# A fused four-stage network kernel: its first attention stage written anew with four heads per step

## What is computed

```python
Q = (x @ WQ_w.T + WQ_b).reshape(b, sq, 16, 16).transpose(0, 2, 1, 3)   # K, V from kv
T = einsum('bhqd,bhkd->bhqk', Q, K) / 4 + attn_bias[:, None]
T = where(mask_i * mask_j == 0, -1e9, T)
out = einsum('bhqk,bhkd->bhqd', softmax(T), V)
x = x + tanh(g_xattn[0]) * (out @ WO_w.T + WO_b)
```

## Time and profile before

| | us |
|---|---|
| median of 3 runs | 2507.8 |
| lowest, highest | 2505.95, 2511.61 |
| the profiled execution | 2495.91 |
| its span | 2493.9 |
| start of A's first scores block | 53.8 |
| B's first load | 469.56 |

### The profile page before, as it was taken

One profiled execution on the slowest core, in us unless ns is written; L12 is line 12 of the kernel. 1 busy time (PEld: TensorE's weight loads), 2 busy tenths in 40 slices (PEclk: granted clock), 3 DMA queues, 4 the chain that ended last, 5 costly groups with the idle time before them and its releaser, 6 DMA issues. The chain is left out here.

```text
span 2493.9 us, 47660 instructions
## 1 busy us (share of the span) xinstructions
PE 2239.0 (90%) x17920; PEld 1548.8 (62%) x18016; DVE 1748.6 (70%) x4970; ACT 879.7 (35%) x2051; POOL 147.6 (6%) x236
## 2 busy tenths in 40 slices
PE   3888888697999999999789999999779999999998
PEld 1555566444475575668445655555568888888887
DVE  4878778476665656553677777777578787878785
ACT  1767567305032131230455555555321111111110
POOL 1623511000000000000000000000000000000000
PEclk8999999799999999999899999999999999999999
DMA  7345233300000000200100000000300000000000
GB/s 195 65 80 88 49 48 48 136 0 1 1 1 1 1 1 1 102 1 1 45 1 1 1 1 1 1 1 1 126 11 1 2 8 0 0 8 0 0 9 9
DMA packets 43512, 65.33 MB, mean 26 GB/s; under 512 B 5056, under 2 KB 36160, under 8 KB 42688
## 3 DMA queue, kind: packets, MB, share of 16 engines
q1 hardware_dynamic: 43328, 62.88, 10.6%
HBM read 54.48 MB, written 8.39 MB: 25 GB/s over the span
## 5 line engine op out<-in xcount | busy, mean ns | idle before, releaser
L2608 PEld LDWEIGHTS banks<-work,big 128*128 128x128 f32 x2048 | 249.7, 194 | 9.7 <-issue 1.9
L2608 PE MATMUL banks<-work,big 128*128 128x128 f32 x2048 | 251.6, 277 | 1.9 <-ACT work L2699 1.7
L2181 PE MATMUL banks<-big,work 128*128 128x256 f32 x1024 | 241.2, 379 | 3.6 <-issue 3.3
L2715 ACT ACTIVATE work<-banks 128x512 f32<-128x512 f32 x128 | 76.5, 598 | 434.1 <-PE banks L2608 434.1
L2107 PE MATMUL banks<-big,work 128*128 128x512 f32 x512 | 221.4, 593 | 0.0
L1791 ACT ACTIVATE work<-banks,work 128x512 f32<-128x512 f32 x256 | 174.1, 686 | 122.0 <-DVE work L1880 121.9
L2181 PEld LDWEIGHTS banks<-big,work 128*128 128x128 f32 x1024 | 195.0, 190 | 33.9 <-issue 1.9
L888 ACT ACTIVATE work<-work 128x512 f32<-128x512 f32 x256 | 182.8, 716 | 83.4 <-DVE work L1026 83.4
L771 PE MATMUL banks<-ident,work 128*128 128x128 f32 x1024 | 161.9, 282 | 49.9 <-ACT work L888 45.2
L1026 DVE CUSTOM_DVE_ANT_0 work<-banks,big 128x512 f32<-128x512 f32 x256 | 173.1, 686 | 38.6 <-issue 34.1
L771 PEld LDWEIGHTS banks<-ident,work 128*128 128x128 f32 x1024 | 122.6, 143 | 83.9 <-ACT work L888 56.1
(11 more groups left out here) (211 smaller groups left out, 3928.0 us busy)
## 6 DMA issues: line engine op xcount, KB each, us to landing
wc<-parts SPq DMA_DIRECT2D x128, 128.0 KB, 6.4
parts<-big SPq DMA_DIRECT2D x16, 384.0 KB, 2.5
big<-in_bias SPq DMA_DIRECT2D x4, 1024.0 KB, 9.7
big<-in_B_val SPq DMA_DIRECT2D x8, 512.0 KB, 6.9
big<-in_B_out SPq DMA_DIRECT2D x1, 4096.0 KB, 19.8
big<-in_D_downT SPq DMA_DIRECT2D x1, 4096.0 KB, 13.8
big<-in_D_up SPq DMA_DIRECT2D x1, 4096.0 KB, 23.1
wc<-in_ctxT SPq DMA_DIRECT2D x1, 2048.0 KB, 7.9
```

Of the source, the lines that this page charges most:

```text
L2181: last = eng.matmul(XO[qt // 2][:, qt % 2 * D:(qt % 2 + 1) * D], spread[:, c % NG, qt * P:(qt + 1) * P], w_out[:, c, :], start=False, stop ...
L2608: last = eng.matmul(HP[n % 2][:, q * P:(q + 1) * P], down[:, kc * ELO + n * NJ + q, :], xnT[par][:, kc, :], start=(kc == 0), stop=(kc == K ...
```

## The change

The prologue block, `cross_attention`, the unused `moe_attention` and `turns` go; `a_attention` takes their place and holds the loads, too. B, C and D are the same but for what they wait on at the start, and the weights of B are loaded inside A. What is new:

- **A step is four heads** of one group at one query tile, so there are 16 steps a batch and 64 in all, with 5 more at the end of the whole stage. All of it is written out, without a hardware loop, and the batches follow one another without a break.
- **Scores in f32 from 16 rows.** Head j of a group lies at partitions 32j to 32j+15 of `qs` and `ks`; four f32 matmuls of 16 rows by 512 columns go to four banks, one row tile each. There is no splitting. SP moves queries and keys of each projection from one SBUF place to another by 16-row strips, 32 KB each, 32 for a batch (`move`).
- **Exp in place, without a row sum.** DVE's instruction writes to `prob`, and ACT works on it there.
- **Transposes of half tiles.** 16 transposes of 64 rows each for a pair of heads fill two banks. ACT copies both banks of the first pair in one instruction (1024 wide), and of the second pair ACT copies one bank and DVE the other.
- **Row sums from ones.** Each head has 32 columns of weights: 16 values and 16 ones. The product has 256 columns, two query tiles; half of a pair's product is made at each step (8 matmuls). Sums come out of the result by 4 small matmuls and go back inverted by 16 (`sums`, `inverses`).
- **One job a step.** Projections, values, outputs, sums and inverses use one bank in turn; `first_slot` places one between the two turns of probabilities, and on four steps of a batch another follows the weighing.
- **The value bias** goes through the output weights once (`constant`) and, with the output bias, into a spare row of them.
- **The root of the norm** is exp(-0.5 ln v), and GpSimd writes the normalised x of batches 1 to 3.

Banks: four for scores, two for transposes, one for weighted values, one for jobs.

```diff
-    turn(0, True)
-    with eng.Fori(1, B - 1) as b:
-        turn(b, True)
-    turn(B - 1, False)
...
-                                left = blocks[tl % 2][0][:, hj, qt * P:(qt + 1) * P]
-                                right = blocks[tl % 2][1][:, hj, :]
...
-                            eng.matmul(SB[step % 2][:, :], left, right, start=True, stop=True).then_inc(s_made.sem, 1)
...
-                            for kt in range(QT):
-                                last = eng.transpose(TB[u % 2][:, kt * P:(kt + 1) * P],
-                                                     prob[:, u % NS, kt * P:(kt + 1) * P], ident[:, :])
-                            last.then_inc(t_made.sem, 1)
...
-                            for kt in kts:
-                                for j in range(A.group):
-                                    h = g * A.group + j
-                                    un = u - A.group + 1 + j
-                                    r = A.strip * j
-                                    last = eng.matmul(OB[g % 2][r:r + A.dk, qt * P:(qt + 1) * P],
-                                                      vtok[:, kt, h * A.dk:(h + 1) * A.dk],
-                                                      pT[:, un % PTR, kt * P:(kt + 1) * P],
...
-                            eng.activation(pT[:, u % PTR, :], TB[u % 2][:, :], ACT.Copy).then_inc(pt_odd.sem, 1)
...
-                            src = sneg[:, step % NS, :] if masked else SB[step % 2][:, :]
-                            done = eng.activation(prob[:, step % NS, :], src, ACT.Exp, bias=low[:, step:step + 1],
-                                                  scale=-1.0 if masked else 1.0, accum_out=rowsum[:, step:step + 1])
...
-                                apart(eng, m)
-                                eng.tensor_tensor_reduce(sneg[:, step % NS, :], SB[step % 2][:, :], bneg[:, qt, :],
-                                                         1.0, 3.0e38, ALU.add, ALU.min, low[:, step:step + 1]
...
-                            eng.tensor_copy(pT[:, u % PTR, :], TB[u % 2][:, :]).then_inc(pt_even.sem, 1)
...
+                def move(whole, spread, job, b, t):
+                    eng.wait_ge(dve_took, TOOK[job])
+                    if b:
+                        eng.wait_ge(s_made, PER * (b - 1) + 2 * QT * (t + 1))
+                    for g in (2 * t, 2 * t + 1):
+                        for j in range(GH):
+                            if b or g:
+                                r = (g % 2 * GH + j) * DK
+                                eng.dma_start(spread[STRIP * j:STRIP * j + DK, g, :], whole[r:r + DK, t, :]
+                                              ).then_inc(strips[g], 16)
...
+                    elif qt == 0:
+                        eng.wait_ge(strips[g], strips_at(b, g))
+                    if n:
+                        eng.wait_ge(low_ready, GH * n)
+                    for j in range(GH):
+                        r = slice(STRIP * j, STRIP * j + DK)
+                        last = eng.matmul(SB[j], qs[r, g, qt * P:(qt + 1) * P], ks[r, g, :], start=True, stop=True)
+                    last.then_inc(s_made, 1)
+                def turn_probs(n, pair):
+                    eng.wait_ge(p_ready, GH * n + 2 * pair + 2)
+                    if pair:
+                        eng.wait_ge(pt_act, 2 * n + 1)
+                    elif n:
+                        eng.wait_ge(pt_act, 2 * n)
+                        eng.wait_ge(pt_dve, n)
+                    for j in range(2):
+                        for kt in range(QT):
+                            for half in range(2):
+                                r, at = slice(half * HALF, (half + 1) * HALF), (j * QT + kt) * HALF
+                                last = eng.transpose(TB[:, half, at:at + HALF],
+                                                     prob[r, n % 2, 2 * pair + j, kt * P:(kt + 1) * P], ident[r, r])
+                    last.then_inc(t_made, 1)
+                def weigh(p, part):
+                    b, g = divmod(p // 2, G)
+                    if part == 0:
+                        eng.wait_ge(pt_act, 2 * (2 * p + 2))
+                        eng.wait_ge(pt_dve, 2 * p + 2)
+                        if p % 2 == 0 and p:
...
+                        eng.wait_ge(ones_made, 2)
+                    for kt in (2 * part, 2 * part + 1):
+                        for j in range(GH):
+                            last = eng.matmul(OB[STRIP * j:STRIP * (j + 1), p % 2 * 2 * P:(p % 2 + 1) * 2 * P],
+                                              vtok[b % 2][:, kt, g * GH + j, :], pT[p % 2][:, j, kt, :],
+                                              start=(kt == 0), stop=(kt == QT - 1))
...
+                for n in range(LAST + 5):
+                    b, i = divmod(n, PER)
+                    if n < LAST:
+                        scores(n)
+                    if 1 <= n <= LAST:
+                        turn_probs(n - 1, 0)
+                    if i % QT == 3 and n >= 7:
+                        sums((n - 7) // QT)
...
+                    if i == 1 and b < B:
+                        queries(b, 1, MB)
...
+                    if 1 <= n <= LAST:
+                        turn_probs(n - 1, 1)
+                    if n >= 3 and (n - 3) // 2 < LAST // 2:
+                        weigh((n - 3) // 2, (n - 3) % 2)
+                    if i == 3 and b + 1 < B:
+                        keys(b + 1, 0, MB)
...
+                def take_pair(n):
+                    eng.wait_ge(t_made, 2 * n + 1)
+                    if n >= 4 and n % 2 == 0:
+                        eng.wait_ge(av_made, n - 2)
+                    at = n % 2 * P
+                    eng.activation(pT[n // 2 % 2][:, 0:2, :, at:at + P].rearrange("p j k (f q) -> p (j k) f q", f=2),
+                                   TB.rearrange("p f (c q) -> p c f q", q=HALF), ACT.Copy).then_inc(pt_act, 1)
+                def take_half(n):
+                    eng.wait_ge(t_made, 2 * n + 2)
+                    at = n % 2 * P
+                    eng.activation(pT[n // 2 % 2][:, 2:4, :, at:at + HALF],
+                                   TB[:, 0, :].rearrange("p (j k q) -> p j k q", j=2, q=HALF), ACT.Copy).then_inc(pt_act, 1)
+                def spread_probs(n, j):
+                    eng.wait_ge(low_ready, GH * n + j + 1)
+                    one = prob[:, n % 2, j, :]
...
+                    if 1 <= n <= LAST:
+                        take_pair(n - 1)
+                    for j in range(2 if n < LAST else 0):
+                        spread_probs(n, j)
+                    if 1 <= n <= LAST:
+                        take_half(n - 1)
+                    if i == 14 and b + 1 < B:
+                        take_values(b + 1, 0, MB)
+                    for j in range(2, GH if n < LAST else 2):
+                        spread_probs(n, j)
...
+                    eng.tensor_tensor_reduce(prob[:, n % 2, j, :], SB[j], bneg[b % 2][:, qt, :], 1.0, 3.0e38,
+                                             ALU.add, ALU.min, low[:, n % 2, j:j + 1]).then_inc(low_ready, 1)
...
+                    for j in range(2 if n < LAST else 0):
+                        lowest(n, j)
+                    if i % QT == 3 and n >= 7:
+                        invert((n - 7) // QT)
+                    for j in range(2, GH if n < LAST else 2):
+                        lowest(n, j)
+                    if 1 <= n <= LAST:
+                        take_half(n - 1)
...
```

More of the change, by code:

```diff
@@ L116, with build @@
 EHI, ELO = 128, 32
-def build(nc, a, out, phases="ABCD"):
+def build(nc, a, out):
     with ExitStack() as ctx:
@@ L128, in build @@
         bank = [banks[:, i, :] for i in range(8)]
-        m = {"phases": phases, "out": out, "stored_tiles": 0, "stores": 0}
+        m = {"out": out, "stored_tiles": 0, "stores": 0}
         m["bank"], m["banks"] = bank, banks
@@ L143, in build @@
         m["work"] = sb("work", [P, 18800])
[L144 removed]
+        s = {n: sem(n) for n in ("x_loaded", "identity_made", "wb_loaded",
                                  "wc_loaded", "c_ctx_loaded", "stored", "dq_loaded", "up_loaded", "x_first_loaded", "scalars_loaded", "scalars_ready")}
         m["s"] = s
[L147 to L155 removed]
+        a_attention(nc, a, m)
+        b_attention(nc, a, m)
+        c_attention(nc, a, m)
+        product_key_experts(nc, a, m)
         epilogue(nc, out, m)
@@ L1719, in project @@
                     last.then_inc(out_made.sem, 1)
-                eng.wait_ge(s["identity_made"], 8)
+                eng.wait_ge(s["identity_made"], 2)
                 eng.wait_ge(s["wc_loaded"], 64)
```

1551 lines of the change are left out of this document (493 added, 1058 removed).

## The result

The changed kernel takes 2441.33 us (median; 2438.86 to 2444.79) beside 2509.7 us for the kernel before on the same chip: a ratio of 0.9725, 95% interval 0.9698 to 0.9752. It is faster by 68 us, where 144 were forecast (2364), and lies above the range, which ended at 2415. Taken again on another occasion, the two gave 2437.34 and 2504.5, a ratio of 0.9731 (0.9707 to 0.9755).

The account below looks back on a forecast made before the run. Stage A was taken as bounded by waits between nearly full PE, DVE and ACT. Start 25 + steps 244 + jobs 44 + end 13 = 326 us against 469.56; 2507.8 - 143.6 = 2364, range 2322 to 2415.

Parts of the forecast that it names:

- The start: Stage A up to the first scores instruction on DVE: 25 us, bounds 21 and 27.
- The base of the step: Stage A, each of 64 steps without its jobs: 3.81 us, 244 us in all where 64 periods before are 300.
- the ring: PE and ACT in turn each step: transposes 0.75, copy 1.10, transposes 0.64, weighing 0.56, scores 0.76; 3.81 us.
- Half transposes and the pair's copy: In each step: first transposes with hand-over 0.75 us, second 0.64, ACT's copy of two banks 1.06.
- Jobs: Projections and other work beside the steps: 11 us a batch, bounds 5 and 16, 44 us for four batches.
- ACT as the fullest engine: Over stage A in the profile after: ACT fullest, near 85% busy, and PE near 75%.
- The turns' 20 us go wholly: Between stage A's turns some 20 us vanish; only the stage's end empties and makes outputs, 13 us, bounds 10 and 15.
- The strips cost nothing on the path: SP's 32 strip moves a batch land in time; if landing takes over 9 us, 3 to 6 us for three batches.
- Row tiles in turn: Rival: the four scores matmuls take turns, 1.93 us instead of 0.76, 75 us more, 2439; chance 0.09.
- A thicker ring: Rival: only two tiles overlap (2386), strips late (2382), or dearer jobs and step 4.05 (2403); chance 0.14 with Changes of shape.
- Changes of shape: Rival: all five tile-shape changes a step cost 0.15 us, not three; 19 us more, 2383; chance 0.14 with A thicker ring.
- The low clock: Rival: TensorE stays at 1.2 GHz in stage A, steps of 7.1 us, 47 us slower than before, 2555; chance 0.04.

Follow-up runs that it names:

- the version with both transfers moved: Changed kernel with the context of batches 1 to 3 and the later masks and biases issued earlier in SP's queue, ahead of strip moves: 2412.74 us, ratio 0.9646.

## Why the prediction was wrong

The sign and the place were right; of 144 us forecast, 68 came. The stage's end was missed by 88 us: 53 from the base of the step, 30 from SP's queue and 7 from the stage's end, less some 2 for the jobs. The time was missed by 11 less, 77 us, and that is luck: the forecast added 11.9 us because the profiled execution of the kernel before was faster than the median, and the one of the kernel after hardly is. Two of the forecast's own signs of error came true, steps that wait for a DMA and a clock below 0.98, but the largest error was in its sum. Step by step:

- **The start** (25 forecast, bounds 21 and 27): 24.82. Right in sum, with luck in the parts. The query strips ran at 14.67 instead of 16, and the four scores matmuls, 1.2 us more, were left out. Keys and queries were counted as half of the matmul records that they leave, but priced at the low clock; they ran at a granted 1.00, 1.72 and 1.81 us where 1.9 was taken.
- **The base of the step** (3.81 forecast): 4.64. This is the step that failed, 64 x 0.83 = 53 us. Two terms of the ring were half of what they should be, for one reason: an f32 matmul stands in the trace as two records. The code issues 4 scores and 8 weighing matmuls, and the rows show x8 and x16. Weighing was taken as 0.56 from a row of "16 matmuls", which is 8 calls; a period before had two such rows (shown below this list), 1.12 in all, and it is 1.01 now (+0.45). Scores were sized by 0.43 for "an f32 matmul of 512 columns", which is half of one. Whole, it occupies 0.86, and the four tiles together 1.07 instead of 0.76 (+0.31). Both numbers came from rows; what was not done is to count the records against the calls in the code. With them the ring is 0.75 + 1.10 + 0.64 + 1.01 + 1.07 = 4.57, and 4.64 was measured.
- **Half transposes and the pair's copy** (0.64 + 0.75 and 1.06): 0.64, 0.71 and 1.02. Right, and with whole transposes 28 us would be gone.
- **Jobs** (11 a batch): 11.7 in a middle batch. The size was right. Most of it is simpler than the list in the forecast: a job of 1.92 us outlasts ACT's copy and makes PE's own program the bound, at 5.27. The projections behind the weighing (1.9 each) and ACT's two table loads, which hold up one pair copy by 1.5 us, are as forecast.
- **ACT as the fullest engine**: wrong. PE is, since its terms were too small; the row sums put back on ACT changed no ordinary step. Its exp without the sum was also taken too low, 0.55: from 25.55 four of them take 2.56 us, so 0.62 from one to the next.
- **The turns' 20 us go wholly**: right, batch follows batch with no gap. The end was short: from the last step's start 17.5 were forecast (one step of 4.5 and 13), and it takes 24.2. Emptying takes 14.0 us up to the output matmuls, where 10.5 were forecast. The 16 output matmuls take 9.44 where 7.17 was taken, at a granted 0.76, with 0.50 in the first 2.4 us. The forecast called the 7.17 the price at the low clock, but the kernel before was granted 1.00 there.
- **The strips cost nothing on the path**: right for the strips, wrong for the queue. The forecast looked at when each strip is needed, and not at what stands behind waiting strips in SP's queue. That cost 29.8 us in three steps, shown by moving the transfers.
- **The rivals.** Row tiles in turn (2439) would have given almost the measured time, and is refuted: one tile takes 3.69 us and four take 1.14. A thicker ring (up to 2403) was nearest in kind, but neither late strips nor a step of 4.05 is what happened. Its 1.11 us for scores of which only two overlap is close to the 1.07 measured, by chance: all four overlap, and each is 0.86 and not 0.43 long. Changes of shape can add at most the 0.07 left over in a step without a job; where a job fills PE they do lie on the path, as the whole transposes showed (1.73 against 1.92), and are part of what is counted as jobs. The 0.15 was also read too high: the 0.49 runs to the next weight load, and to the next matmul it is 1495.33 - 1494.78 = 0.55. The low clock was not the rule, but it was no bystander: 0.92 over the stage.

Timeline of the kernel before, the two rows of weighing between the scores instructions at 412.73 and 417.41:

```profile
413.05 0.63 PE L795 MATMUL banks<-work,big 128*16 128x128 f32 x16
...
416.41 0.63 PE L795 MATMUL banks<-work,big 128*16 128x128 f32 x16
```

Set right with the numbers of the version with both transfers moved, the sum is 25 + 64 x 4.64 + 41.6 + (24.3 - 4.6) = 383 without the queue's stalls; 41.6 is all that its 63 steps take beyond 63 x 4.64, some 4 us at the lower clock among it. As its terms come from that trace, it shows only that none is missing (382.98 there). By the forecast's count the time would be 2507.8 - (469.56 - 383) = 2421, where 2412.7 was measured, and with 30 us of stalls 2451 for the changed kernel, where 2441 was measured. That 8 and 10 us are too many fits the 11.9 that the forecast had added, but the median of the kernel before also differs from chip to chip (2501.0 beside that version), so this is not shown.

The best kernel here without less exact arithmetic is the version with both transfers moved, 24 to 29 us under the changed kernel. The one with the four idle matmuls can't be told from it.

## What to carry to other kernels

Before a duration per matmul is taken from a group, count its records against the calls in the code: a factor of two in the terms of a ring was most of the error here. When transfers that wait for late work join a queue, list what stands behind them in that queue and who waits for it; their own slack says nothing of that. And where two late transfers meet in one stall, move both before judging either.

## What the runs showed of the hardware that was not expected

- An f32 matmul of 512 columns is two records and holds PE for 0.86 us; four of 16 rows in four row tiles hold it for 1.07 up to the next instruction. An f32 transpose of 64x64 is one record, x16 for 16 calls. A job whose tile shape is that of the transposes beside it holds PE for 1.73 us, with another shape beside it for 1.92.
- Less work on PE can lose the clock and with it the gain. bf16 weighing took the stage from a granted 0.92 to 0.78 (0.97 to 0.82 with the transfers moved), and the same matmuls issued three times brought back 0.95 and 14.6 us. But full work doesn't hold it either: with the scores in one row tile PE was busy for 646 of 662 us at 0.72. Which property of PE's work decides is open.
- A piece of 3 us in which PE was busy for 1.79 was followed by at least 9 us at 1.2 GHz with PE full; one short matmul in each of four steps kept it at 2.4 GHz there.
